# Attention with relative positions on one core: the last relative step before the softmax's last lo halves, its copies before the last transfer of probabilities

## The reference

```python
x = x + attention(group_norm(x))          # x: (64, 14, 14, 768), 12 heads of 64, 196 tokens an image

qkv = x @ qkv_w.T + qkv_b                 # q and v also get a rank-4 term: x @ la.T @ lb.T
attn = einsum('bqd,bkd->bqk', q * scale, k)
rel_h = einsum('bhwc,hkc->bhwk', r_q, Rh)  # Rh = rel_pos_h[i - j + 13], one 14 x 14 table per axis
rel_w = einsum('bhwc,wkc->bhwk', r_q, Rw)
attn = softmax(attn + rel_h[..., None] + rel_w[..., None, :])
out = einsum('bqk,bkd->bqd', attn, v) @ proj_w.T + proj_b
```

## Time and profile before

| | |
|---|---|
| median of 3 runs | 3377.29 us |
| the profiled execution | 3377.3 us |
| its span | 3375.5 us |
| PE busy | 3255.6 us, 96% |
| DVE busy | 2533.7 us, 75% |
| ACT busy | 2068.8 us, 61% |
| DMA queue of SP, share of 16 engines | 48.8% |

### The profile page before, as it was taken

How to read it: one execution, slowest core, us unless ns; L and a number is a source line. 1 busy time by engine, 2 the same in 40 slices (tenths; PEclk the granted TensorE clock), 3 DMA queues, 4 the chain that set the end, 5 groups by cost and what they waited for, 6 DMA issues and landing times.

```text
span 3375.5 us, 80210 instructions
## 1 busy us (share of the span) xinstructions
PE 3255.6 (96%) x31984; PEld 2145.2 (64%) x31984; DVE 2533.7 (75%) x5970; ACT 2068.8 (61%) x5651; POOL 35.7 (1%) x65
## 2 busy tenths in 40 slices
PE   7689999999999999999999999999999999999997
PEld 4456666666666666666666666666666666666664
DVE  7577777777777777777777777777777777777764
ACT  2466666666666666666666666666666666666653
POOL 0000000000000000000000000000000000000000
PEclk9899999999999999999999999999999999999999
DMA  3145655555565555555555565555565555555554
GB/s 127 42 90 108 124 113 105 121 114 106 122 125 105 113 118 107 114 121 105 117 114 114 107 125 108 111 119 114 110 122 121 101 120 113 107 121 122 105 102 102
DMA packets 1091412, 376.13 MB, mean 111 GB/s; under 512 B 916696, under 2 KB 1071320, under 8 KB 1091040
## 3 DMA queue, kind: packets, MB, share of 16 engines
q1 hardware_dynamic: 1075206, 333.63, 48.8%
q10 hardware_dynamic: 15834, 37.37, 3.9%
HBM read 86.60 MB, written 38.54 MB: 37 GB/s over the span
## 4 chain that ended last, share of the span: by engine, by line
PE 76%; DVE 5%; ACT 5%; DMA 5%; SPq 4%; issue 2%; POOL 0%; DVEq 0%; POOLq 0%
PE ring L570 45%; PE ring L636 11%; PE ring L612 8%; PE ring L626 6%; ACT prob L695 3%; DMA turned<-split 2%; DMA rel_q<-rel_sb 2%; SPq L518 2%; PE ring L592 2%; PE ring L642 2%; DVE split L802 2%; PE ring L650 2%; SPq L541 1%; DVE rel_sb L775 1%; DVE rel_sb L769 1%
## 5 line engine op out<-in xcount | busy, mean ns | idle before, releaser
L570 PE MATMUL ring<-xn_hi,w_hi 128*128 128x392 f16 x3456 | 1142.4, 331 | 7.7 <-DVE xn_lo L852 4.5
L570 PE MATMUL ring<-xn_lo,w_hi 128*128 128x392 f16 x3456 | 1140.4, 330 | 0.0
L570 PE MATMUL ring<-xn_hi,w_lo 128*128 128x392 f16 x3456 | 1140.3, 330 | 0.0
L695 ACT ACTIVATE prob<-ring,neg_max,exp_scale 98x196 f32<-98x196 f32 x1536 | 768.5, 515 | 306.2 <-DVE neg_max L786 306.2
L802 DVE SCALAR_TENSOR_TENSOR split<-prob,row_inv,split 98x196 f16<-98x196 f32 x1536 | 545.4, 418 | 8.7
L782 DVE TENSOR_REDUCE row_max<-ring 98x4 f32<-98x784 f32 x384 | 373.0, 971 | 186.5 <-PE ring L612 180.6
L570 PEld LDWEIGHTS ring<-xn_hi,w_hi 128*128 128x128 f16 x3456 | 342.4, 99 | 246.9 <-DVE xn_lo L852 4.6
L570 PEld LDWEIGHTS ring<-xn_hi,w_lo 128*128 128x128 f16 x3456 | 338.5, 98 | 236.7 <-issue 2.3
L570 PEld LDWEIGHTS ring<-xn_lo,w_hi 128*128 128x128 f16 x3456 | 338.8, 98 | 215.9 <-issue 1.9
L636 PE MATMUL ring<-o_hi,w_hi 128*128 128x392 f16 x1152 | 381.5, 331 | 9.9 <-DVE k_lo L749 7.9
L636 PE MATMUL ring<-o_lo,w_hi 128*128 128x392 f16 x1152 | 380.5, 330 | 0.0
(11 more groups left out here) (118 smaller groups left out, 4885.2 us busy)
## 6 DMA issues: line engine op xcount, KB each, us to landing
y_sb<-in_x SPq DMA_DIRECT2D x192, 196.0 KB
out<-y_sb SPq DMA_DIRECT2D x192, 196.0 KB
x_sb<-in_x ACTq DMA_DIRECT2D x31, 1176.0 KB
rel_q<-rel_sb SPq DMA_DIRECT2D x128, 122.5 KB, 2.5
stage<-in_L_conv_qkv_w SPq DMA_DIRECT2D x3, 2304.0 KB, 15.4
turned<-split SPq DMA_TRANSPOSE x384, 4.1
rel_q<-rel_sb SPq DMA_DIRECT2D x128, 24.5 KB, 2.3
v_tok<-v_split SPq DMA_TRANSPOSE x192, 3.3
```

The costliest lines, as they stand in the source:

```text
L570: last = T.matmul(ring[:, bank, 0:NT], w[:, c, 128 * j:128 * j + 128], xx[:, par, c, :], start=(c == 0 and part == 0), stop=(c == CT - 1 a ...
L695: last = A.activation(prob[:, k % 2, head, half, :], score[0:HALF, k % 2, head, TOK * half:TOK * half + TOK], ACT.Exp, bias=neg_max[:, k % ...
```

## The change

Three of the five lists change, each in one place; PE's and POOL's don't. No instruction is added or removed.

```diff
 ACT_ORDER:
-    + each("N", 0, 11) + each("R", -1, 3) + each("T", 0, 11) + each("Y", 1, 4) + each("R", -1, 4) + each("K", -1, 0)
+    + each("N", 0, 11) + each("R", -1, 3) + each("T", 0, 11) + each("R", -1, 4) + each("Y", 1, 4) + each("K", -1, 0)
 DVE_ORDER:
-    + each("N", 0, 11) + each("R", -1, 3) + each("T", 0, 11) + each("R", -1, 4) + each("Z", 1, 3) + each("K", -1, 0)
+    + each("N", 0, 11) + each("R", -1, 3, 4) + each("T", 0, 11) + each("Z", 1, 3) + each("K", -1, 0)
 SP_ORDER:
-    + each("T", 0, 10) + each("VT", 0, 5) + each("T", 0, 11) + each("CA", -1, 0) + each("ST", 1, 3) + each("LY", 1, 5))
+    + each("T", 0, 10) + each("VT", 0, 5) + each("CA", -1, 0) + each("T", 0, 11) + each("ST", 1, 3) + each("LY", 1, 5))
```

## The result

The changed kernel takes 3347.9 us (median of 4 runs, 3346.3 to 3352.5), the kernel before 3376.3 us beside it: a ratio of 0.9918, 95% interval 0.9901 to 0.9935. That is 28 us less (22 to 33 by the interval), where 24.5 were forecast. The profiled execution took 3346.98 us, 30.3 less than that of before.

What follows compares the result with a forecast made beforehand. PE, busy 96% of the span, and its idle gaps were taken as the time. From 3377.3 us, - 24.8 - 1.8 + 2.1 gave 3352.8 us; own range 3349 to 3358 us, 8 in 10 range 3346 to 3367 us.

Steps and rivals of the forecast that it cites:

- term 1: Later pair boundaries: S 0's whole wait on PE for the copies goes at each of 30, -24.8 us.
- rival D: More gained: clock stays up in first turn, K 0 in time, S 0 and S 1 faster; 3346 us, chance 0.10.
- term 3: Y 5 on PE waits 0.07 us longer for K 0's lo half from DVE, 30 times: +2.1 us.
- term 2: First turn: S 0's wait of 5.63 us shrinks as the copies start earlier, -1.8 us.
- T 11 (no cost): Moved transfer, issued behind the copies on SP, still lands 1.15 us before P 11 needs it: no cost.
- rival A: T 11 lands a little late for P 11, 0.42 us at each boundary; 3366 us, chance 0.12.
- rival C: Slower: T 11's data held up long behind copies, store and load, so P 11 waits; 3407 us at 7 us, chance 0.05.
- DVE has P 0 as its next reader on PE, over 10 us away: Loads behind T 11: if LY 5 comes late for Z 5 on DVE, PE loses nothing.
- Rival B: Gain doesn't stay, or S 0's wait was not for the copies; 3377.6 us, chance 0.08.

Runs made afterwards that it cites:

- e1_sp_only: Kernel before with only SP's list changed: copies CA ahead of transfer T 11, DVE and ACT in their old orders; 3395.8 us, ratio 1.0067.
- e3_no_act: Changed kernel with ACT's old order, Y 4 ahead of R 4; 3377.0 us, ratio 0.9999.
- e4_k0_first: Changed kernel with K 0's lo half ahead of Z 3 on DVE; 3340.6 us, ratio 0.9890.
- e8_first_turn: Kernel before with the change's new order in the first turn alone, the old one in the 31 others; 3370.4 us, ratio 0.9989.
- b2_same: Kernel before once more, no edit, one execution for a second trace; 3372.8 us.
- e5_t11_later: Changed kernel with transfer T 11 behind store ST 3 and load LY 5 on SP; 3368.2 us, ratio 0.9985.
- e2_no_sp: Changed kernel with SP's old list, T 11 ahead of the copies; DVE's and ACT's changes stay; 3440.4 us, ratio 1.0190.

## Why the prediction was right, and what it missed

*The gap of S 0 (term 1, -24.8 us): right.* It is gone in all 30 later turns, and the intermediate times fit. The times of the boundary can be laid over those of the trace before by the end of R 3 on DVE (1543.15 and 1531.96, 11.19 apart): R 4 was put at 1543.25 and starts at 1543.28; the copies were put at 1544.48 and start at 1544.46. What was missed is that their own time would shrink too: from the first issue to the last landing it was 4.82 us, and is now 4.36 (the last of the four is issued at 1535.12 and lands 2.51 us later; the expectation of e1_sp_only put it at 4.15). With the 0.5 us by which the copies start earlier in e1_sp_only, that is enough for the gap of S 0 to go there too.

*The size of term 1: too small by some 2 us.* PE's busy time in the 29 turns fell by 2.3 us, and the sum held nothing for it. Under rival D it was put down to the scores, which would run 1.48 us instead of 1.55. They do not run faster. From the start of S 0 to the start of P 10 it is 1.48 us before (1552.89 - 1551.41) and 1.47 after (1541.01 - 1539.54), and PE's busy time in the scores' line L612, over the same 29 turns, is the first number behind the length of the stretch, before and then after:

```profile
342.00:3253.36 2911.36, 269.51 (x5568) 234.86 (x5568) 1.00 0.55 114
```

```profile
342.30:3227.90 2885.60, 269.44 (x5568) 233.94 (x5568) 1.00 0.56 115
```

The 1.55 us of the chain count from the start of S 0 to the end of its last matmul, where a chain without a wait counts from the end of the step before. What changed is the end of Z 4: it stood by itself before the wait, and S 0 now starts within it, some 0.07 us a turn, 2 us in 29. So the row of idle time gave a little less than a boundary had to win. P's waits for transfers are 2.3 us less as well; no run tells whether that is the change or chance (in the second traces the difference is 1.2 us).

*K 0 (term 3, +2.1 us): right in kind.* 0.10 us a turn, 2.9 in all. e3_no_act and e4_k0_first move this wait by +0.56 and -0.30 us and the time follows, in e3_no_act by more than the wait, since the clock falls in 6 turns.

*The first turn (term 2, -1.8 us): right in sign, its size open.* S 0 waited 1.6 us in both traces of the changed kernel, where 3.8 were forecast. How long it waits hangs on the clock ahead of it too: where the clock did not fall between 185 us and the wait, it was 5.63 us in the kernel before and 3.3 in e3_no_act and e8_first_turn; where it fell twice there, PE came later, and the waits were 4.0 us in the kernel before (b2_same) and 1.6 in the changed one. Like with like, the wait shrinks by 2.3 or 2.4 us and not by 1.8, and the 0.5 us between are those by which the copies' own time shrank. What the wait gives back in time is less sure: e8_first_turn says 3.7 us with an interval from 0.7, and the first two turns took 155.6 and 160.5 us in two traces of the changed kernel.

*T 11 (no cost): right, and rival A falls.* It lands 4.0 to 5.1 us after its issue in the 29 turns; the point from which it costs was put at 5.25, so the cover was as thin as said. e5_t11_later shows rival C's mechanism at work once T 11 is pushed further: 6.2 us to landing in one turn, a time 20 us worse.

*The step that was wrong though it cost nothing here:* "DVE has P 0 as its next reader on PE, over 10 us away". The late load of LY 5 holds Z 5, and X 5 stands in its PSUM bank 2 us later. The row that was read (four waits of DVE for such loads) told that there was slack, not how much: about 0.6 us after the change. e1_sp_only crosses that line and is slower than the kernel before.

*Rival B* (the gain is given back) falls: of 25.8 us in 29 turns 23.5 are PE's idle time.

*Forecast or rival D?* The measured 3347.9 us lie just below the forecast's own range (3349 to 3358) and nearer to rival D's 3346. But D's three reasons did not come true as they were given: K 0 was not in time, the scores do not run faster, and in the first turn the clock fell at other places. The path of the forecast is the one that the traces show, with term 1 some 2 us too small and term 2 perhaps as much, and a small part of the nearness to D is luck.

## What to carry to other kernels

Where one engine is busy nearly all the time, a move is judged by its gaps turn by turn; for each DMA issue that a move delays, find all who read its data and all who take the PSUM bank of that reader, and measure the slack of each. The three parts of this change are not worth a third each: SP's move alone loses some 20 us, DVE's and ACT's alone lose 64, together they win 28. And a gap of TensorE can cost 1.6 to 2 us more than its length, when the clock falls behind it.

## What the runs showed of the hardware

In the middle turns of the twelve traces the granted clock fell 26 times to its lower level, and each time within 3.5 us of the start of a wait of PE of 0.85 us or more. Behind the 238 waits of 0.25 to 0.84 us there was no fall, the 0.30 us of Y 5 in the changed kernel among them. Behind the 29 waits of Y 5 of 0.86 us (e3_no_act) there were 6, behind the 29 of S 0 of 1.9 us and more (e2_no_sp) 13. Length is not all: none of the 31 waits of 0.9 to 1.3 us was followed by one, and in the kernel before none of S 0's waits was, up to 1.6 us. What decides between them, no run has tried. A fall behind a short wait cost 1.6 to 2 us. In the first two turns, where PE waits more, two traces of one kernel differ by 5 us, with the granted clock differing and the program not.

A transfer of probabilities, T 11 over 29 turns, lands 4.0 us after its issue in the kernel before (4.0 to 4.6), 4.1 us (4.0 to 5.1) behind four copies of 122.5 KB, and 4.8 us (4.3 to 6.3) when a store and a load of 196 KB stand between as well. The four copies themselves take 3.04 us to issue right behind a transfer and 2.44 us without one.
